# Similarity weights of the block builder over two chunks of nodes at once

## The reference, cut to what matters

```
Wh = h @ W + b
dot = sum(Wh[row] * Wh[col]);  sim = dot / max(|Wh[row]| * |Wh[col]|, EPS)
base = adj_v * softplus(deg_coeff[0] * deg_v + deg_coeff[1]) * (row != col)
prop_pos = segment_sum((base * relu(sim))[:, None] * Wh[col], row)
prop_neg = segment_sum((base * -relu(-sim))[:, None] * Wh[col], row)
out = scale * (c[0] * prop_pos + c[1] * prop_neg + c[2] * Wh)
```

## Time and profile before

| | |
|---|---|
| median of three runs | 1847.92 us (1847.14 to 1849.7) |
| the profiled execution | 1844.67 us, its span 1843.0 us |
| busy in the span | PE 1153.8 us, DVE 1161.9, ACT 458.6, POOL 125.3 |
| granted TensorE clock, mean of the span | 0.794 |

### The profile page before, as it was taken

One profiled execution on the slowest core, in us unless ns is written; L12 is line 12 of the kernel. 1 busy time (PEld: TensorE's weight loads), 2 busy tenths in 40 slices (PEclk: granted clock), 3 DMA queues, 4 the chain that ended last, 5 costly groups with the idle time before them and its releaser, 6 DMA issues. The chain is left out here.

```text
span 1843.0 us, 38373 instructions
## 1 busy us (share of the span) xinstructions
PE 1153.8 (63%) x16508; PEld 977.7 (53%) x16508; DVE 1161.9 (63%) x2153; ACT 458.6 (25%) x1133; POOL 125.3 (7%) x215
## 2 busy tenths in 40 slices
PE   0000231677777877777787777547564767589997
...
DMA packets 40247, 146.66 MB, mean 80 GB/s; under 512 B 24156, under 2 KB 24700, under 8 KB 33276
## 3 DMA queue, kind: packets, MB, share of 16 engines
...
...
## 5 line engine op out<-in xcount | busy, mean ns | idle before, releaser
L1065 PE MATMUL b_ps<-b_u_b,b_y 128*128 128x64 f32 x1250 | 207.8, 317 | 112.1 <-DVE k_xs L1028 106.5
L1065 PEld LDWEIGHTS b_ps<-b_u_b,b_y 128*128 128x128 f32 x1250 | 192.4, 233 | 131.5 <-DVE b_y L1022 128.5
L1232 PE MATMUL gcn_ps<-c_u,c_c 128*128 128x192 bf16 x1875 | 160.6, 250 | 117.2 <-PEq L85 77.3
L1065 PE MATMUL b_ps<-b_mv,b_soh 64*128 64x50 bf16 (+1 forms) x9600 | 221.1, 206 | 18.4 <-DVE b_mv L1006 12.9
L1232 PEld LDWEIGHTS gcn_ps<-c_u,c_c 128*128 128x128 bf16 x1875 | 159.3, 100 | 118.4 <-issue 77.8
L1065 PEld LDWEIGHTS b_ps<-b_mv,b_soh 64*128 64x128 bf16 x9600 | 196.1, 107 | 42.4 <-DVE b_mv L1006 13.9
L927 ACT ACTIVATE b_c_row<-b_ps 128x300 bf16<-128x300 f32 (+1 forms) x275 | 115.4, 420 | 408.6 <-PE b_ps L1065 407.3
L1006 DVE TENSOR_TENSOR b_mv<-b_mv,b_two 128x468 bf16<-128x468 bf16 (+1 forms) x600 | 179.5, 367 | 0.0
L1111 PEld LDWEIGHTS b_ps<-k_ident,b_a_row 128*128 128x128 f32 x625 | 81.3, 165 | 150.9 <-issue 93.6
L1111 PE MATMUL b_ps<-k_ident,b_a_row 128*128 128x128 f32 x625 | 129.5, 335 | 49.4 <-DVE b_scale L1014 49.4
L1014 DVE SCALAR_TENSOR_TENSOR b_scale<-head_rn_row,head_cap,b_ps 128x512 f32<-128x512 f32 (+1 forms) x175 | 120.3, 687 | 60.4 <-PE b_ps L1111 59.7
...
## 6 DMA issues: line engine op xcount, KB each, us to landing
...
```

The source lines that it names most:

```text
L1065: return nc.tensor.matmul(out, lhsT, rhs, start=start, stop=True, skip_group_check=True)
L1232: return nc.tensor.matmul(out, lhsT, rhs, start=start, stop=True, skip_group_check=True)
```

## The change

Sim, `pos` and y are made for a group of two chunks (1024 columns) at a time; the seven chunks are four groups, 0 and 1, 2 and 3, 4 and 5, and 6 alone. The scale remains an instruction per chunk, since bank 6 is there once. The two chunks' products write side by side into bank 7, and one addition of eight columns of 64 (512 numbers) takes both out. Similarity passes signal once per group, and the Relu on ACT covers banks 4 and 5 in one instruction.

The one-hot encoding is split in two entries: "hi", the first compare (L1002 before), and "hot", the rest. The lists are rewritten. In `VORDER` the "hi" of the next group stands between the second scale and y, and the rest of that one-hot group behind y. In `ORDER` both products of a group stand before the next group's passes and transposes.

Three scratch tiles of the stage's head (`rel`, `qt`, `rest`) now lie in y's buffers, which are twice as large, and the accumulating DMAs of later rounds are issued at another place of POOL's stream.

```diff
+NG = (NC + 1) // 2
-ORDER = [("lot", 0), ("lot", 1), ("chunk", 0), ("lot", 2), ("lot", 3), ("chunk", 1), ("prop", 0), ("lot", 4), ("chunk", 2),
-         ("prop", 1), ("lot", 5), ("chunk", 3), ("prop", 2), ("lot", 6), ("chunk", 4), ("prop", 3), ("lot", 7), ("lot", 8),
...
+ORDER = [("lot", 0), ("chunk", 0), ("lot", 1), ("chunk", 1), ("lot", 2), ("prop", 0), ("lot", 3), ("prop", 1), ("chunk", 2),
+         ("lot", 4), ("chunk", 3), ("lot", 5), ("prop", 2), ("lot", 6), ("prop", 3), ("chunk", 4), ("lot", 7), ("chunk", 5),
+         ("lot", 8), ("lot", 9), ("chunk", 6), ("prop", 4), ("lot", 10), ("prop", 5), ("prop", 6)]
-        pos = [l.sb(f"pos{i}", [P, 512]) for i in range(2)]
+        pos = l.sb("pos", [P, 1024])
-        y = [l.sb(f"y{i}", [P, 512]) for i in range(2)]
+        y = [l.sb(f"y{i}", [P, 1024]) for i in range(2)]
+        rel, qt, rest = y[0][:, 0:512], y[0][:, 512:1024], y[1][:, :].rearrange("p (a n) -> p a n", a=2)
+        both = lambda g: ps[:, SIM:SIM + 2, :] if wide(g) == 1024 else ps[:, SIM, 0:wide(g)]
...
-                nc.scalar.activation(pos[i % 2][:, 0:P * nh], ps[:, SIM + i % 2, 0:P * nh], ACT.Relu,
-                                     scale=coef[:, 0:1]).then_inc(s["pos"], 1)
+                nc.scalar.activation(side(pos, g), both(g), ACT.Relu, scale=coef[:, 0:1]).then_inc(s["pos"], 1)
...
+            def similar(v, g):
+                dve.wait_ge(s["made"], NG * v + (g + 1))
+                dve.wait_ge(s["pos"], NG * v + (g + 1))
+                nc.vector.scalar_tensor_tensor(side(sim[g % 2], g), both(g), coef[:, 1:2], side(pos, g),
                                                ALU.mult, ALU.add).then_inc(s["sgn"], 1)
+            def weigh(v, g):
+                n = wide(g)
+                dve.wait_ge(s["propped"], NC * v + (2 * NC + (2 * g - 1 if g >= 2 else g)))
+                dve.wait_ge(s["sgn"], NG * v + (g + 2))
+                dve.wait_ge(s["scaled"], NC * v + (min(2 * g + 2, NC) + 1))
+                nc.vector.tensor_tensor(y[g % 2][:, 0:n], sim[g % 2][:, 0:n], scale[g % 2][:, 0:n], ALU.mult).then_inc(s["made"], 1)
+            def add(v, g):
+                h0, n = CHUNKS[2 * g][0], wide(g) // P
+                dve.wait_ge(s["propped"], NC * v + (2 * NC + 1 + min(2 * g + 2, NC)))
...
             def propagate(v, par, i):
-                pe.wait_ge(s["made"], NC * v + (i + 3))
-                pe.wait_ge(s["added"], NC * v + (i + 1))
+                pe.wait_ge(s["made"], NG * v + (g + 3))
+                pe.wait_ge(s["added"], NG * v + (g + 1))
```

More of the change, by code:

```diff
@@ L756, in build @@
         gate_at, zero16, zero = l.sb("gate_at", [P, 1]), l.sb("zero16", [P, 1], BF16), l.sb("zero", [P, 1])
-        pos = [l.sb(f"pos{i}", [P, 512]) for i in range(2)]
+        pos = l.sb("pos", [P, 1024])
         begun = l.sb("begun", [P, 6])
-        sim, scale = [l.sb(f"sim{i}", [P, 512]) for i in range(2)], [l.sb(f"scale{i}", [P, 512]) for i in range(2)]
-        y = [l.sb(f"y{i}", [P, 512]) for i in range(2)]
+        sim, scale = [l.sb(f"sim{i}", [P, 1024]) for i in range(2)], [l.sb(f"scale{i}", [P, 1024]) for i in range(2)]
+        y = [l.sb(f"y{i}", [P, 1024]) for i in range(2)]
+        rel, qt, rest = y[0][:, 0:512], y[0][:, 512:1024], y[1][:, :].rearrange("p (a n) -> p a n", a=2)
         ps = l.ps("ps", [P, 8, 512])
@@ L768, in build @@
         SIM, AT, PR = 4, 6, 7
+        wide = lambda g: P * sum(CHUNKS[i][1] for i in range(2 * g, min(2 * g + 2, NC)))
+        side = lambda tile, g: (tile[:, 0:1024].rearrange("p (a n) -> p a n", a=2) if wide(g) == 1024
+                                else tile[:, 0:wide(g)])
+        both = lambda g: ps[:, SIM:SIM + 2, :] if wide(g) == 1024 else ps[:, SIM, 0:wide(g)]
         again = lambda r: not isinstance(r, int)
@@ L860, in first @@
                     double(r * NB, 0, o)
-                if again(r):
-                    add_out(r, 0, 0)
                 double(r * NB + 1, 1, 0)
@@ L884, in _, with end @@
             pool.wait_ge(s["gate"], 5)
-            plan(pool, head, first, step, lambda r: None, widen)
+            def end(r):
+                if again(r):
+                    add_out(r, NB - 1, 0)
+            plan(pool, head, first, step, end, widen)
         @block.sync
@@ L954, in step @@
                         evacuate(r, w, par, i)
-                    if what == "chunk":
-                        positive(w - 1, i)
+                    if what == "chunk" and i % 2 == 0:
+                        positive(w - 1, i // 2)
             def end(r):
-                for i in range(NC):
-                    positive(r * NB + (NB - 1), i)
+                for g in range(NG):
+                    positive(r * NB + (NB - 1), g)
             nc.scalar.activation(begun[:, 4:5], k["ones"][:, 0:1], ACT.Copy).then_inc(s["evac"], 6)
@@ L997, in onehots @@
                 twice = lambda q, m: two[b][:, q, 0:n, None, :].to_broadcast([P, n, m // 2, 2])
-                dve.wait_ge(s["doubled"], 4 * w + (o + 1))
-                dve.wait_ge(s["lot"], NL * w + (ENDS[o - 2] + NL if o >= 2 else ENDS[o + 2]))
                 hi = halves(mv[b][:, 0:n, 2, :])
-                nc.vector.tensor_tensor(hi, nums(HI), twice(0, HI), ALU.is_equal).then_inc(s["hot"], 1)
+                if part == "hi":
+                    dve.wait_ge(s["doubled"], 4 * w + (o + 1))
+                    dve.wait_ge(s["lot"], NL * w + (ENDS[o - 2] + NL if o >= 2 else ENDS[o + 2]))
+                    nc.vector.tensor_tensor(hi, nums(HI), twice(0, HI), ALU.is_equal).then_inc(s["hot"], 1)
+                    return
                 nc.vector.tensor_tensor(halves(soh[b][:, 0:n, :]), nums(P), twice(1, P), ALU.is_equal)
@@ L1024, in add @@
-            def add(v, i):
-                h0, nh = CHUNKS[i]
-                dve.wait_ge(s["propped"], NC * v + (2 * NC + i + 2))
-                part = prop[:, h0:h0 + nh, :]
-                nc.vector.tensor_tensor(part, part, ps[:, PR, 0:nh * F].rearrange("p (h f) -> p h f", f=F),
-                                        ALU.add).then_inc(s["added"], 1)
+                nc.vector.scalar_tensor_tensor(scale[g % 2][:, lo:lo + n], rn_row[:, P * h0:P * h0 + n], cap[:, bass.ds(b, 1)],
+                                               ps[:, AT, 0:n], ALU.min, ALU.mult).then_inc(s["scaled"], 1)
@@ new lines, in add, with weighing @@
+            def add(v, g):
+                h0, n = CHUNKS[2 * g][0], wide(g) // P
+                dve.wait_ge(s["propped"], NC * v + (2 * NC + 1 + min(2 * g + 2, NC)))
+                part = prop[:, h0:h0 + n, :]
+                nc.vector.tensor_tensor(part, part, ps[:, PR, 0:n * F].rearrange("p (h f) -> p h f", f=F), ALU.add).then_inc(s["added"], 1)
+            def weighing(v, b, what, i):
+                if what == "scale":
+                    scaling(v, b, i)
+                if what == "sim":
+                    similar(v, i)
+                if what == "y":
+                    weigh(v, i)
+                if what == "add":
+                    add(v, i)
@@ L1097, in chunk @@
                 h0, nh = CHUNKS[i]
+                g = i // 2
                 if i == 0:
@@ L1143, in end @@
                         propagate(r * NB + (NB - 1), 0, i)
-            for name, n in (("lot", NL), ("sims", 2 * NC), ("at", 2 * NC), ("propped", 2 * NC + 1)):
+            for name, n in (("lot", NL), ("sims", NG), ("at", 2 * NC), ("propped", 2 * NC + 1)):
                 mm(ps[:, 7, 0:2], k["zeros16"][:, 0:P], k["zeros16"][:, 0:2], True).then_inc(s[name], n)
```

84 lines of the change are left out of this document (38 added, 46 removed).

## The result

The changed kernel took 1972.05 us (median of four runs, 1971.02 to 1974.45) against 1848.35 (1847.14 to 1849.7) of the kernel before: a ratio of 1.0671, 95% interval 1.0652 to 1.0689. That is 124 us slower, where 66 were forecast, and 2 us above the upper end of the range. A second set of runs of the same kernel gave 1974.14 and 1.0684. The profiled execution took 1972.61 us, 1970.9 of it span; its clock is 0.749.

What follows compares the result with a forecast made beforehand. PE and DVE were taken as a relay, each nearly full. A step of 24.1 + 6.05 + 6.6 = 36.7 us against 34.1 adds 62 us over 24 steps, the last block 4: 1914 us, range 1812 to 1970.

Steps and rivals of the forecast that it cites:

- What bounds it: In the block stage, PE and DVE work as a relay, each nearly full, in a step of 34.1 us.
- What DVE saves: Wider instructions and another instruction in place of waits save DVE some 1.8 us per step (0.8 and 1.0).
- What the order puts between: PE's work between y and the next scale's transposes, twice a step: 4.4 us at upper clock, 7.7 at lower.
- Which clock: Idle stretches lower PE's clock, so its two stretches behind y take 6.05 and 6.6 us; the step 36.7.
- passage 1: PE's work from y0 to transpose 2: product 0, lot 3, product 1, two similarity passes, transposes; taken as 6.05 us.
- passage 2: The same PE work from y1 to transpose 4, first product at the high clock, rest low; taken as 6.6 us.
- the all-low rival: PE's clock stays low through both stretches behind y; a step of 39.5 us, 1986 us in all; chance 0.20.
- After the last step: The last block, without one-hots to fill waits, takes 31 us instead of 27.0, so +4.
- The clock stays up: Rival: upper clock through both PE stretches behind y; steps of 32.6 to 33.9 us, 1810 us; chance 0.20.
- the point of decision: If PE's two stretches between y and the next transposes total under 10.0 us, the kernel is faster.
- DVE is all that counts: Rival: DVE's other work covers PE, so DVE's starts set the step, 28.4 us; 1711 us; chance 0.05.
- What would show it: Signs in the new profile: POOL's copies 36 to 37.5 us apart, DVE waiting before scales 2 and 4, clock 0.75 or under.

Runs made afterwards that it cites:

- both chunks ahead: The changed kernel with chunk 2's passes and transposes moved ahead of product 0 in PE's list and chunk 4's ahead of product 2; 1722.59 us, ratio 0.9318.
- two fills: The changed kernel with matmuls of zeros put ahead of PE's waits for y before products 0 and 2; 1833.74 us, ratio 0.9935.
- the last but one kernel: The changed kernel with chunks 2 and 4 ahead of products, compares behind y, and POOL's doubling of one-hot group 1 ahead of its copies; 1707.62 us, ratio 0.9254.
- the halved y: The changed kernel with each 1024-column y made by two instructions of 512, each product waiting for its own half; 1915.48 us, ratio 1.0390.

## Why the prediction was wrong in size

**What bounds it** was right: a relay between two nearly full engines, decided by what PE has to do between a y and the next transposes. With just that taken out, both chunks ahead, the kernel lost 9.5 us a step.

**What DVE saves**: 1.8 us a step forecast in starts. The three stretches without passages came to 8.63 + 4.53 + 10.43 = 23.6 us in the step shown (the mean of the 22 is the same), forecast were 9.0 + 4.6 + 10.06 = 23.7. The term holds, though its parts were not all as I had them: idle time ahead of y was 13.6 us in the whole kernel before and is 0.1 now, 0.6 us a step where I had 1.0. On the rule of the Trainium skill, "VectorE: DVE Perf Modes", section "The DRAIN you can't avoid": the rows still differ from it, since where y directly follows its scale it starts 0.86 us behind it, and the compare 0.65 (both chunks ahead, without and with the compare between). But putting work there gained nothing in time.

**What the order puts between**: the content of both passages and their prices were right. At the upper clock 4.60 us with the 0.2 around it (forecast 4.6), at the lower 8.09 (forecast 7.9).

**Which clock** is the step that failed. I took 6.05 and 6.6 us for the passages, the one half high, the other with its first product high, after one row of the kernel before. Without the 0.2 around them they came out at 7.24 and 7.48 in the mean of 22 steps (6.9 and 7.9 in the step shown): at most the first product and a part of the lot behind it are high, and from the second product on everything is low. That is 2.1 us a step, all of the step's 38.76 against 36.7, and over 24 steps 50 us of the 58 by which I was short.

The waits of PE were not what I had wrong. Ahead of passage 1 I had 1.6 us and ahead of passage 2 2.3; the 22 steps have 1.7 to 2.0 and 2.0 to 2.4. What I had wrong is what such a wait does to the clock. The pattern for passage 2 was the product at 768.81, which stays high after a wait of 1.21 us; in the kernel before that is the exception. Its product 2 waits 1.21 us in all 22 steps, and in 21 of them it runs low (1.94 us); only the one shorter step has it high. For passage 1 I took the middle between the two levels without a row for it. The measured step lies near the all-low rival (39.5), to which I gave 0.20.

Nor does a longer step feed itself through longer waits: PE's waits ahead of the two passages stay within those bounds in steps of 37.2 to 39.9 us, and its idle time is 8.1 to 8.5 us in those under 38 and 7.2 to 8.1 in those over 39. Why product 0 is high after 2.0 us of waiting in one step and low after as much in another stays open.

**After the last step** I took 31 us for 25.5 to 35.5; it is 33.9, so I was 3 us short for the same reason: two passages at the lower clock, waits of 6.89 us.

**The rivals.** "The clock stays up" was forecast at 32.6 us a step or more; with two fills the shortest steps take 32.4 us, and the kernel is then faster than before, as the point of decision said (both passages under 10.0 together: 8.8 in such a step, 9.7 in the mean). "DVE is all that counts" was put at 28.4 us a step and 1711 us. With both chunks ahead of the products, and nothing else, the kernel comes near it, 29.2 and 1723; that the last but one kernel hits it, 28.35 and 1708, is partly luck, as it also has POOL earlier. So what held the change back is its order, which puts the products ahead of the transposes. The rule of "Perfetto Trace Analysis" in the Trainium skill, section "Optimizing Scalar/DVE Operations", pointed the right way, and the halved y shows it: more instructions on DVE, 59 us less.

**What would show it**: copies 36 to 37.5 us apart (38.8), scale 2 waiting 3.2 us (4.3 in the mean) and scale 4 4.7 (5.7), four waits of PE for products (there), the clock at 0.75 or under (0.66), and DVE busy some 1 us less a step (1.6). All came in the forecast direction; the step and the waits were forecast too small by the clock.
